# A graph network on one core: in the attention pass, six short operations go to GpSimd and the later stages are delayed by a step

## The reference

```python
Wr, Wc = Wh[row], Wh[col]
dot = jnp.sum(Wr * Wc, axis=-1)
nr, nc = norm(Wr), norm(Wc)
sim = dot / jnp.maximum(nr * nc, EPS)
sim_pos, sim_neg = relu(sim), -relu(-sim)
base = adj_v * softplus(...) * (row != col)
prop_pos = segment_sum((base * sim_pos)[:, None] * Wc, row)
prop_neg = segment_sum((base * sim_neg)[:, None] * Wc, row)
out = scale * (coeff[0] * prop_pos + coeff[1] * prop_neg + coeff[2] * Wh)
```

## Time and profile before

| what | us |
|---|---|
| median of three runs (10889.98 to 10927.57) | 10903.28 |
| the profiled execution, its own time | 11012.01 |
| span of its trace | 11009.5 |
| attention pass in the trace, 3545 to 5672 | 2127 |
| in this stretch: DVE busy | 1955.8 |
| in this stretch: PE busy | 1821.0 |
| in this stretch: ACT busy | 1258.4 |
| in this stretch: POOL busy | 0 |

### The profile page before, as it was taken

How to read it: one execution, slowest core, us unless ns; L and a number is a source line. 1 busy time by engine, 2 the same in 40 slices (tenths; PEclk the granted TensorE clock), 3 DMA queues, 4 the chain that set the end, 5 groups by cost and what they waited for, 6 DMA issues and landing times. The chain is left out here.

```text
span 11009.5 us, 264222 instructions
## 1 busy us (share of the span) xinstructions
PE 8013.0 (73%) x91323; PEld 7303.2 (66%) x91323; DVE 6560.1 (60%) x19944; ACT 3764.4 (34%) x6989; POOL 3294.7 (30%) x3251
## 2 busy tenths in 40 slices
PE   5466566666666888888879998999646666666656
PEld 5244455555555888888868997999545555555556
DVE  2699232232333899999978995999434443444444
ACT  1000122222222556656546774777211111111111
POOL 0686555555540000000000000000055555555552
PEclk9866677777775999999979997999656666666666
DMA  4321111111111322222212331333211010100101
GB/s 53 43 50 44 49 52 50 52 49 52 50 43 43 93 85 84 84 85 84 85 46 86 98 98 45 99 98 98 36 20 18 18 19 18 18 18 18 19 18 22
DMA packets 650582, 589.26 MB, mean 54 GB/s; under 512 B 392902, under 2 KB 496422, under 8 KB 649960
## 3 DMA queue, kind: packets, MB, share of 16 engines
q1 hardware_dynamic: 545816, 464.32, 15.4%
q0 software_dynamic: 104272, 117.41, 5.0%
HBM read 541.80 MB, written 39.60 MB: 53 GB/s over the span
## 5 line engine op out<-in xcount | busy, mean ns | idle before, releaser
L765 POOL DMA_INDIRECT soft_G<-soft,soft_idx x1568 | 1518.5, 968 | 1422.1 <-ACT soft_idx L852 921.6
L765 POOL DMA_INDIRECT msg_G<-msg_src,msg_idx x1176 | 1162.4, 988 | 1047.7 <-ACT msg_idx L852 704.6
L1677 ACT ACTIVATE sage_G<-ps 128x384 bf16<-128x384 f32 (+1 forms) x2650 | 1284.7, 485 | 502.0 <-PE ps L1688 495.4
L642 POOL MEMSET acc<- 96x1280 f32 x30 | 34.4, 1163 | 4648.6 <-POOLq L1290 2470.6
L1688 PE MATMUL ps<-T,sage_ohT 128*128 128x192 bf16 x10388 | 1304.5, 247 | 18.0 <-DVE sage_ohT L1645 17.3
L1700 PE MATMUL ps<-sage_G,sage_ohd 128*128 128x192 bf16 x10388 | 1286.5, 245 | 0.3 <-issue 0.3
L1651 DVE TENSOR_SCALAR sage_ohd<-iota,sage_cols 128x256 bf16<-128x256 bf16 x5194 | 1137.5, 279 | 95.3 <-PE ps L1700 63.4
L1533 PE MATMUL ps<-att_far,att_ohT 128*128 128x65 bf16 x15582 | 948.0, 197 | 319.6 <-DVE att_ohT L1484 268.4
L1533 PEld LDWEIGHTS ps<-att_far,att_ohT 128*128 128x128 bf16 x15582 | 695.4, 100 | 385.5 <-DVE att_ohT L1484 270.6
L1533 PE MATMUL ps<-acc,att_ohT 128*128 128x65 bf16 x15582 | 943.3, 197 | 0.8 <-issue 0.8
L1688 PEld LDWEIGHTS ps<-T,sage_ohT 128*128 128x128 bf16 x10388 | 904.2, 98 | 31.2 <-DVE sage_ohT L1645 18.1
(11 more groups left out here) (441 smaller groups left out, 16517.3 us busy)
## 6 DMA issues: line engine op xcount, KB each, us to landing
sage_rows<-srow SPq DMA_DIRECT2D x424, 320.0 KB, 3.3
acc<-pair_rows SPq DMA_DIRECT2D x196, 448.0 KB, 3.7
att_rows<-pair_rows SPq DMA_DIRECT2D x147, 448.0 KB, 3.6
msg_edge<-edge_attr SPq DMA_DIRECT2D x196, 256.0 KB
sage_rows<-srow SPq DMA_DIRECT2D x106, 288.0 KB, 3.3
soft_G<-soft,soft_idx POOLq DMA_INDIRECT x1568
msg_G<-msg_src,msg_idx POOLq DMA_INDIRECT x1176
kept_rows<-acc POOLq DMA_DIRECT2D x49, 256.0 KB
```

What stands on the lines that cost most here:

```text
L642: done(pool.memset(acc[0:TOP, nodes], 0.0), "zeroed")
L765: eng.indirect_dma_start(B["G"][h][:, j, :], None, src_table, bass.IndirectOffsetOnAxis(ap=B["idx"][h][:, j:j + 1], axis=0)).then_inc(gath ...
L1677: act.activation(G[s % RING][:, 0:m, :], ps[:, s % RING, 0:m * 3 * D].rearrange("p (c n) -> p c n", c=m), ACT.Copy).then_inc(S["taken"], 1)
```

## The change

The last part of `dve_weight` leaves DVE. DVE keeps the product, the guard, the sum and the reciprocal (`dve_dot`). GpSimd does the rest in a new stage `pool_weight`, with six operations in place of four: maximum and minimum of the sum with zero, each times its coefficient, their sum, and that times the reciprocal. `prod` and `t` get a second buffer. The lags are new, too: V is made a step later than the dot product, everything behind V moves by one, and so do `pe_flip` and `act_one_hots`. `pe_flip` now stands ahead of `pe_gather`.

```diff
-                        prod = left[:, RW:RW + PC * W65].rearrange("p (c d) -> p c d", d=W65)
-                        t, weight, red = buf("t", [P, 6, PC], F32, 1)[0], buf("weight", [P, PC], F32, 4), buf("red", [P, 2, D], F32, 1)[0]
+                        t, weight, red = buf("t", [P, 6, PC]), buf("weight", [P, PC], F32, 4), buf("red", [P, 2, D], F32, 1)[0]
+                        prod = [left[:, RW:RW + PC * W65].rearrange("p (c d) -> p c d", d=W65), buf("prod", [P, PC, W65], F32, 1)[0][:]]
...
-                        def dve_weight(dve, i, s):
+                        def dve_dot(dve, i, s):
                             b, q, n, m = place(i, s)
-                            k = s // QS
-                            mine = own[k][:, :, q * PC:q * PC + m]
                             dve.wait_ge(S["taken"], n + 1)
-                            dve.tensor_tensor(prod[:, 0:m, :], ps[:, s % 2, 0:m * W65].rearrange("p (c d) -> p c d", d=W65), C_[s % 4][:, 0:m, :], ALU.mult).then_inc(S["prod"], 1)
+                            need(dve, S["weight"], n - 1)
+                            dve.tensor_tensor(prod[s % 2][:, 0:m, :], ps[:, s % 2, 0:m * W65].rearrange("p (c d) -> p c d", d=W65), C_[s % 4][:, 0:m, :], ALU.mult).then_inc(S["prod"], 1)
                             dve.wait_ge(S["prod"], n + 1)
-                            dve.tensor_scalar(t[:, 0, 0:m].rearrange("p (c o) -> p c o", o=1), prod[:, 0:m, D:W65], 1.0e-8, None, ALU.max).then_inc(S["guard"], 1)
-                            dve.tensor_reduce(t[:, 1, 0:m], prod[:, 0:m, 0:D], AX, ALU.add).then_inc(S["dot"], 1)
+                            dve.tensor_scalar(t[s % 2][:, 0, 0:m].rearrange("p (c o) -> p c o", o=1), prod[s % 2][:, 0:m, D:W65], 1.0e-8, None, ALU.max).then_inc(S["guard"], 1)
+                            dve.tensor_reduce(t[s % 2][:, 1, 0:m], prod[s % 2][:, 0:m, 0:D], AX, ALU.add).then_inc(S["dot"], 1)
                             dve.wait_ge(S["guard"], n + 1)
-                            dve.reciprocal(t[:, 2, 0:m], t[:, 0, 0:m]).then_inc(S["recip"], 1)
-                            dve.wait_ge(S["dot"], n + 1)
-                            dve.wait_ge(S["recip"], n + 1)
-                            dve.tensor_tensor(t[:, 3, 0:m], t[:, 1, 0:m], t[:, 2, 0:m], ALU.mult).then_inc(S["sim"], 1)
-                            dve.wait_ge(S["sim"], n + 1)
-                            dve.scalar_tensor_tensor(t[:, 4, 0:m], t[:, 3, 0:m], 0.0, mine[:, 0, :], ALU.max, ALU.mult).then_inc(S["pos"], 1)
-                            dve.scalar_tensor_tensor(t[:, 5, 0:m], t[:, 3, 0:m], 0.0, mine[:, 1, :], ALU.min, ALU.mult).then_inc(S["neg"], 1)
-                            dve.wait_ge(S["pos"], n + 1)
-                            dve.wait_ge(S["neg"], n + 1)
-                            need(dve, S["v"], n - 3)
-                            dve.tensor_tensor(weight[s % 4][:, 0:m], t[:, 4, 0:m], t[:, 5, 0:m], ALU.add).then_inc(S["weight"], 1)
+                            dve.reciprocal(t[s % 2][:, 2, 0:m], t[s % 2][:, 0, 0:m]).then_inc(S["recip"], 1)
+
+                        def pool_weight(pool, i, s):
+                            b, q, n, m = place(i, s)
+                            u, mine = t[s % 2], own[s // QS][:, :, q * PC:q * PC + m]
+                            if q == 0:
+                                pool.wait_ge(S["block"], b + 1)
+                            pool.wait_ge(S["dot"], n + 1)
+                            hold(pool)
+                            pool.tensor_scalar(u[:, 3, 0:m], u[:, 1, 0:m], 0.0, None, ALU.max).then_inc(S["over"], 1)
+                            pool.tensor_scalar(u[:, 4, 0:m], u[:, 1, 0:m], 0.0, None, ALU.min).then_inc(S["under"], 1)
+                            pool.wait_ge(S["over"], n + 1)
+                            pool.tensor_tensor(u[:, 3, 0:m], u[:, 3, 0:m], mine[:, 0, :], ALU.mult).then_inc(S["pos"], 1)
+                            pool.wait_ge(S["under"], n + 1)
+                            pool.tensor_tensor(u[:, 4, 0:m], u[:, 4, 0:m], mine[:, 1, :], ALU.mult).then_inc(S["neg"], 1)
+                            pool.wait_ge(S["pos"], n + 1)
+                            pool.wait_ge(S["neg"], n + 1)
+                            pool.tensor_tensor(u[:, 5, 0:m], u[:, 3, 0:m], u[:, 4, 0:m], ALU.add).then_inc(S["both"], 1)
+                            pool.wait_ge(S["both"], n + 1)
+                            pool.wait_ge(S["recip"], n + 1)
+                            need(pool, S["v"], n - 3)
+                            pool.tensor_tensor(weight[s % 4][:, 0:m], u[:, 5, 0:m], u[:, 2, 0:m], ALU.mult).then_inc(S["weight"], 1)
 
                         def dve_add(dve, i, s):
                             b, q, n, m = place(i, s)
@@ -1572,7 +1582,7 @@
 
                             @block.vector
                             def _(dve):
-                                flow(dve, (0, dve_turned), (3, dve_rest), (4, dve_lo), (6, dve_add), (1, dve_weight), (1, dve_v))
+                                flow(dve, (0, dve_turned), (4, dve_rest), (5, dve_lo), (7, dve_add), (2, dve_v), (1, dve_dot))
                                 dve.drain()
                                 next_slots(dve)
 
@@ -1580,11 +1590,15 @@
                             def _(act):
                                 act.wait_ge(cols_in, 16)
                                 act_block(act, 0, 0)
-                                flow(act, (2, act_hi), (1, act_one_hots), (3, act_mid), (0, act_take), (0, act_next))
+                                flow(act, (3, act_hi), (2, act_one_hots), (4, act_mid), (0, act_take), (0, act_next))
+
+                            @block.gpsimd
+                            def _(pool):
+                                flow(pool, (1, pool_weight))
 
                             @block.tensor
                             def _(pe):
-                                flow(pe, (5, pe_sum), (0, pe_gather), (0, pe_flip))
+                                flow(pe, (6, pe_sum), (1, pe_flip), (0, pe_gather))
 
                         with nc.Block() as block:
                             @block.sync
```

More of the change, by code:

```diff
@@ L1368, in att_slots @@
                 S = {n: scope.enter_context(nc.semaphore(f"att_{n}")) for n in
-                     "block ohT flip0 flip1 ohs0 ohs1 gathered taken prod dot guard recip sim pos neg weight v hi rest mid lo summed red added".split()}
+                     "block ohT flip0 flip1 ohs0 ohs1 gathered taken prod dot guard recip over under both pos neg weight v hi rest mid lo summed red added".split()}
                 rows_in = [scope.enter_context(nc.semaphore(f"att_rows_in{k}")) for k in range(4)]
```

## The result

The changed kernel takes 11344.62 us (median of 4 runs, 11335.64 to 11361.22) against 10907.28 us (4 runs) of the kernel before: ratio 1.040, 95% interval 1.0376 to 1.0425, 437 us more. Forecast were 307 us more, 11210, with a range up to 11330. The direction and the kind of loss came as forecast, its size did not. The profiled execution has a span of 11350.0 us. That is only 340.5 more than the 11009.5 of before, whose profiled execution lies 105 us above its median; in the two traces the pass, from the first gathers to the end of the last, grew by 432 us (3549.9 to 5660.6 before, 3471.1 to 6014.3 now), so nearly the whole loss lies in it.

The account below looks back on a forecast made before the run. DVE was taken to bound the attention pass before, and a ring of gathers, ACT's copies and flips after. The ring's 273 us and the clock's 34 make 307 more than 10903.3: 11210 us, range 11090 to 11330.

Parts of the forecast that it names:

- What bounds before, and that DVE ceases to be the bound: Attention pass: DVE, 93% busy, sets 42.70 us a block before; afterwards DVE near 80% busy, PE not waiting for its one-hots.
- The ring: Gathers, ACT's copies and flips wait for each other in turn: 48.27 us a block, 273 us more; 80% as forecast.
- The later one counts: ACT's one-hot copy waits for both hi (G + 1.24) and PE's sum (G + 1.36), G being the sum's start.
- First copy 1.02, hand-over to PE 0.05: From the start of ACT's first one-hot copy to PE's first flips, at 2.43 us after the sum's start.
- position 0 has only eight flips ahead (2.87 + 2.70 = 5.57): A block's first step on PE: only eight flips precede its gathers, so it takes 5.57 us, where full steps take 6.18.
- one such stretch per block now ... I take half of the blocks, 34 us: PE's clock falls after long waits, slowing gathers by 1.41 us: 0 to 69 us more, 34 us taken.
- The clock stays low: Rival, 4%: PE's clock never rises again, steps take about 8.2 us, time 11990 us.
- no change: Rival, 3%: the ring is 5.6 us a block shorter than reckoned, time 10903 us.
- GpSimd the bound: Rival, 6%: GpSimd's six operations need over 4.4 us a step, time 11576 us.
- The other edits at nothing: DVE's delays, GpSimd's six operations (1.7 us, within 3.9 us of cover) and SP's loads add no time.
- The ring doesn't hold: Rival, 7%: one-hot copies are done when PE reaches the flips; DVE's 36.0 us a block counts, time 10575 us.
- the upper bound of the prediction: Each of GpSimd's six operations waits out one DVE instruction: 5.4 us a step, 400 us more.

Follow-up runs that it names:

- e1: Changed kernel with the flips behind the gathers again, one-hot copies at a lag of 1, sum at 5: 0.982 of the kernel before.
- e3: Changed kernel with one-hot copies at a lag of 1 and the sum at 5, flips still ahead of the gathers: 0.988 of the kernel before.
- e9: Kernel before with only the changed order and lags of ACT and PE, and rest, lo, add a step later on DVE: 1.044 of the kernel before.
- e8: Changed kernel with ACT's hi copy behind the one-hot copies and the sum at a lag of 5: 1.015 of the kernel before.
- e7: Changed kernel with ACT's hi copy behind the one-hot copies instead of ahead of them: 1.043 of the kernel before.
- e6: Changed kernel with four blocks instead of two in an iteration of the pass's loops: 1.038 of the kernel before.
- e4: Changed kernel with 57 more semaphore instructions on PE ahead of the pass: 1.041 of the kernel before.
- e2: Changed kernel with the whole weight made on DVE again and GpSimd idle, all lags kept: 1.038 of the kernel before.
- e10: Repetition of e1 on another chip (changed kernel with the flips behind the gathers again): 0.976 of the kernel before.

## Why the prediction was right in kind and wrong in size

- *What bounds before, and that DVE ceases to be the bound*: right (no wait for its one-hots). DVE's share is 69%; "near 80%" was forecast.
- *The ring*: right, link for link, and shown from three sides. Opening it turns the loss into a gain (e1, e3), closing it alone in the kernel before gives the whole loss (e9), and taking the two middle links out shortens a step by 0.72 us (e8; 0.64 reckoned), while taking out hi alone does nothing for a full step (e7). "The later one counts" held.
- *The step "First copy 1.02, hand-over to PE 0.05"*: the release from ACT to PE took 0.15 (4508.29 to 4508.44), not the 0.05 taken from DVE to PE. With the other links the gaps between gathers are longer by 0.48 a block than reckoned, 23 us.
- *The step "position 0 has only eight flips ahead (2.87 + 2.70 = 5.57)", taken for all 49 blocks*, is the one that failed. Its price holds in the middle of an iteration: 2.97 us from a block's last gathers to the next block's first, and 2.69 for these. Across the edge between two iterations, which the prediction names nowhere (it leaves out only "the prologue and epilogue"), it is 6.21 and 4.36 (the gaps are medians, the gathers' time is a mean, over the 25 and 23 such places of the trace). The gap makes 1.65 a block on average, 81 us, and the gathers behind it 0.75 a block, 37 us. Before, an edge made a block 0.3 us longer, since DVE's pace covered a branch of 0.45; in the changed kernel the branch takes 2.64, and it lies in the ring. e6 takes half of the edges away and gets 63 us back; e4 shows that the wait is bound to the code's place and not to the block's data.
- *The step "one such stretch per block now ... I take half of the blocks, 34 us"*: the stretch is the one at position 5, and its price was near. The gathers there were slow in 20 of 45 blocks and take 3.23 us on average in place of 2.69, 0.54 x 49 = 26 us. That "half" came so close was luck, since no row gave it. There are two such stretches, and the second is the one behind the edge.
- The sum: 273 + 23 + 26 + 81 + 37 = 440, measured 437; without the edge's 118 it would be 322, and the time within the range. The edge could have been found in the trace of before, by PE's branch row (0.45 us, shown above), though not that it would grow to 2.64; a reader of the earlier trace rows alone can't see it, since no step shown there crosses an edge.
- *The other edits at nothing*: right. Six operations of GpSimd took 1.4 us (1.7 reckoned), and e2 and e9 show that neither they nor V's delay counts while the ring holds. Where DVE is busier they took longer (the last section).
- *The clock stays low*, *no change*, *GpSimd the bound*: none came. *The ring doesn't hold* came only where it was opened on purpose. There DVE's 36.0 was too low a price: PE's own 35.1 and the 78.0 us that it waits for lo (1.6 a block) make 36.7 of e1's 37.87. The rest was not taken apart.

The Trainium skill (Runtime: NRT & Kernel Launch, "Instruction fetch mechanics") says that a taken branch whose target isn't in the window held by the engine makes it fetch the code before it can go on. A wait at the edge, its independence of data and its count agree (e4, e6); that in e4 it comes 11 matmuls behind the edge is more than that sentence says. That the wait is such a fetch is therefore likely and not shown. Why it was 0.45 us before and 2.64 after in a loop of nearly the same length is not shown by any run here.

## What to carry to other kernels

Before a stage is moved by one step, write down for each engine what it needs of the step before, and look for a closed ring. A stage that was hidden behind long work (here the gathers) is bare when it is moved to the other side of that work, and then every hand-over, every wait at a loop's edge and every fall of the clock counts in full. When a forecast moves the bound to another engine, read that engine's rows over one whole iteration, edge and branch included, and not over steps in the middle of it.

## What the runs showed of the hardware

GpSimd's small operations take longer when DVE is busy. Groups of GpSimd by line, 3600 to 4600, in the changed kernel (DVE at 69%) and in e10 (DVE at 94%), mean ns behind the comma:

```profile
L1513 POOL TENSOR_TENSOR att_t<-att_t 128x7 f32<-128x7 f32 (+1 forms) x154 | 31.4, 204 | 22.1
```

```profile
L1513 POOL TENSOR_TENSOR att_t<-att_t 128x4 f32<-128x4 f32 (+1 forms) x213 | 90.5, 425 | 30.6
```

The six together go from 1.31 to 2.24 us by their means, and single ones of e10 reach 1.47. In the changed kernel they cost nothing that e2 could tell; in e10 DVE waits 16.6 us of 1500 for the weight, and no run tells what that costs. So the upper bound of the prediction was not empty. The Trainium skill's rule that the two engines shut each other out (SBUF — State Buffer, "Who interferes with whom") agrees in kind; no run tested it as the cause. A wait of PE at a loop's edge, 2.3 to 3.0 us in the branch at 22 of 23 edges of the changed kernel, which e4 moves into the middle of a sum whose data are there, was the other thing not expected.
